# Two output biases of a four-stage transformer kernel: from a VectorE addition to a one-row TensorE product

## What is computed

```python
def _L0_xattn_ref(q, k, v, ...):          # 16 heads, an extra position term in the scores ("cope")
    ...
    return out @ Wo_w.T + Wo_b
def _L1_xattn_ref(q, kv, ...):            # 16 heads, plain
    ...
    return out @ w_out + b_out
...
x = x + tanh(g_xattn[0]) * _L0_xattn_ref(layernorm(x), ctx, ctx, ...)
x = x + tanh(g_ffn[0])   * _L0_ffn_ref(layernorm(x), ...)
x = x + tanh(g_xattn[1]) * _L1_xattn_ref(layernorm(x), ctx, ...)
x = x + tanh(g_ffn[1])   * _L1_ffn_ref(layernorm(x), ...)
```

## Time and profile before

| | us |
|---|---|
| median of 3 runs | 4901.44 |
| lowest and highest | 4898.19, 4908.12 |
| the profiled execution | 4907.68 |
| its span, first to last instruction | 4906.0 |
| VectorE busy in it | 3975.6 (81%) |
| TensorE busy in it | 3332.2 (68%) |
| ScalarE busy in it | 2426.4 (49%) |
| GpSimd busy in it | 1394.9 (28%) |

### The profile page before, as it was taken

One profiled execution on the slowest core, in us unless ns is written; L12 is line 12 of the kernel. 1 busy time (PEld: TensorE's weight loads), 2 busy tenths in 40 slices (PEclk: granted clock), 3 DMA queues, 4 the chain that ended last, 5 costly groups with the idle time before them and its releaser, 6 DMA issues.

```text
span 4906.0 us, 64542 instructions
## 1 busy us (share of the span) xinstructions
PE 3332.2 (68%) x21126; PEld 2210.1 (45%) x21126; DVE 3975.6 (81%) x8619; ACT 2426.4 (49%) x5505; POOL 1394.9 (28%) x1125
## 2 busy tenths in 40 slices
PE   3347677676767767676776767767676766767686
PEld 2125344453544436354453635435354443635363
DVE  3699787887978879787888978888797887978753
ACT  2464555545555454554545455554554545455432
POOL 0242322323232232322323232232323223232300
PEclk7558687686877778687786867778687777868687
DMA  4000000000000000000000000000000000000000
GB/s 130 13 5 1 1 12 1 11 1 1 12 1 12 1 11 1 1 12 1 11 1 3 10 1 12 1 11 1 1 12 1 12 1 11 1 1 7 1 7 3
DMA packets 42692, 40.93 MB, mean 8 GB/s; under 512 B 6469, under 2 KB 42343, under 8 KB 42361
## 3 DMA queue, kind: packets, MB, share of 16 engines
q1 hardware_dynamic: 42360, 36.85, 2.5%
HBM read 32.64 MB, written 4.19 MB: 8 GB/s over the span
## 4 chain that ended last, share of the span: by engine, by line
DVE 42%; PE 26%; ACT 13%; issue 13%; POOL 2%; DVEq 0%; POOLq 0%; ACTq 0%; DMA 0%; SPq 0%
DVE banks L731 7%; DVE u L962 5%; PE banks L288 4%; DVE row_negmax L1273 4%; PE banks L366 3%; PE banks L275 3%; DVE masks L722 3%; PE banks L297 3%; DVE eg_eth L980 3%; DVE c L689 3%; DVE o L989 2%; PE banks L330 2%; DVE steps L749 2%; PE banks L810 2%; ACT core_prob L581 2%
## 5 line engine op out<-in xcount | busy, mean ns | idle before, releaser
L731 DVE COPY_PREDICATED banks<-masks,banks 128x448 f32<-128x448 int16 (+5 forms) x1536 | 1030.6, 671 | 36.6
L632 POOL TENSOR_TENSOR steps<-slope,rises 128x512 f32<-128x512 f32 x256 | 301.3, 1177 | 2373.9 <-DVE masks L722 2162.0
L810 PE MATMUL banks<-xn,w 128*128 128x256 f16 x6912 | 876.7, 290 | 74.6 <-ACT h L882 50.0
L810 PEld LDWEIGHTS banks<-xn,w 128*128 128x128 f16 x6912 | 704.9, 104 | 239.4 <-ACT h L882 58.2
L689 DVE TENSOR_TENSOR_SCAN c<-gate,cap 128x514 f32<-128x514 f32 x256 | 371.0, 1449 | 83.6 <-POOL neg_rest L642 82.4
L1273 DVE TENSOR_REDUCE row_negmax<-banks 128x4 f32<-128x1024 f32 x256 | 297.3, 1216 | 154.5 <-PE banks L351 151.9
L722 DVE TENSOR_SCALAR masks<-shift 128x512 int16<-128x512 int16 x1536 | 334.3, 288 | 89.8 <-ACT shift L558 85.6
L823 PE MATMUL banks<-w,a 128*128 128x256 f32 x1152 | 303.6, 411 | 85.3 <-DVE o L989 79.0
L646 POOL TENSOR_TENSOR partial<-partial,core_scores 128x512 f32<-128x512 f32 x256 | 361.4, 1412 | 0.1
L642 POOL TENSOR_TENSOR neg_rest<-shift,c 128x512 f32<-128x512 bf16 x256 | 293.5, 1146 | 219.6 <-ACT shift L570 144.5
L882 ACT ACTIVATE h<-banks,b 128x256 f32<-128x256 f32 x576 | 239.8, 467 | 198.3 <-PE banks L810 197.3
(11 more groups left out here) (262 smaller groups left out, 7493.4 us busy)
## 6 DMA issues: line engine op xcount, KB each, us to landing
stage<-in_L_ffn_w SPq DMA_DIRECT2D x16, 512.0 KB, 5.5
ahead<-in_ctx SPq DMA_DIRECT2D x32, 128.0 KB, 2.2
ahead<-in_x SPq DMA_DIRECT2D x32, 128.0 KB, 2.3
u<-in_ctx SPq DMA_DIRECT2D x32, 128.0 KB
x<-in_x SPq DMA_DIRECT2D x32, 128.0 KB
out<-x SPq DMA_DIRECT2D x32, 128.0 KB, 1.8
stage<-in_L_ffn_w SPq DMA_DIRECT2D x8, 256.0 KB, 6.1
stage<-in_L_ffn_sw SPq DMA_DIRECT2D x2, 512.0 KB, 4.4
```

Source lines behind the costliest of these rows:

```text
L731: move = nc.vector.copy_predicated(tab[:, :, 0:S - b], k.masks[:, n, :, 0:S - b], tab[:, :, b:S])
L810: last = nc.tensor.matmul(k.bank[bank][:, f * S:(f + 1) * S], w[:, e, a, c, par, f * P:(f + 1) * P], k.x_parts[:, b, c, :], start=(n == 0) ...
```

## The change

`token_projection` can now add a bias in PSUM: after the two products of a token tile it multiplies a stationary operand of one row and 128 columns (`half[0:1, 0:1]`, the constant 0.5, broadcast) with the first row of the bias tile (1 x 256), accumulating into the same bank. That is two further products in float32 for each call, for cope and for cross, 64 in all 32 calls. `add_to_x` loses its second instruction. The bias rows of these two stages are scaled by 2.0 ahead of the batches, in place of the tanh, so that 0.5 times the row is the bias, and the tanh comes in with the first instruction of `add_to_x`, which multiplies the whole bank by it. The gated stage keeps its bias on VectorE.

```diff
-def token_projection(nc, w, src, bank):
+def token_projection(nc, w, src, bank, ones=None, row=None):
     for t in range(NT):
         for c in range(NC):
             last = nc.tensor.matmul(bank[:, t * D:(t + 1) * D], src[:, c, t * P:(t + 1) * P], w[:, c, :],
-                                    start=(c == 0), stop=(c == NC - 1))
+                                    start=(c == 0), stop=(c == NC - 1 and row is None))
+        if row is not None:
+            last = nc.tensor.matmul(bank[:, t * D:(t + 1) * D], ones[0:1, 0:1].broadcast_to([1, P]), row[0:1, :],
+                                    start=False, stop=True)
     return last
...
-    token_projection(nc, k.wo_cope, k.oT, k.bank[7]).then_inc(sem["tail_y_done"], 1)
+    token_projection(nc, k.wo_cope, k.oT, k.bank[7], k.half, k.bo_cope).then_inc(sem["tail_y_done"], 1)
...
-    add_to_x(nc, k, step, k.bank[7], k.tanh_g[:, 0:1], k.bo_cope)
+    add_to_x(nc, k, step, k.bank[7], k.tanh_g[:, 0:1])
...
-def add_to_x(nc, k, step, bank, scale, bias_row):
+def add_to_x(nc, k, step, bank, scale):
     x = k.norm.x
     step(nc.vector.scalar_tensor_tensor(whole(x), bank[:], scale, whole(x), ALU.mult, ALU.add))
-    step(nc.vector.tensor_tensor(x[:], x[:], bias_row[:].unsqueeze(1).broadcast_to([P, NT, D]), ALU.add))
...
-    token_projection(nc, w.wo, k.oT, k.bank[7]).then_inc(sem[p + "y_done"], 1)
+    token_projection(nc, w.wo, k.oT, k.bank[7], k.half if kind == "cross" else None,
+                     w.tbo if kind == "cross" else None).then_inc(sem[p + "y_done"], 1)
...
-        add_to_x(nc, k, step, k.bank[7], k.tanh_g[:, 1:2], w.tbo)
+        add_to_x(nc, k, step, k.bank[7], k.tanh_g[:, 1:2])
...
-                for n, b in ((0, k.bo_cope), (1, k.bo_cross), (3, k.bo_gated)):
-                    nc.vector.tensor_scalar(b[:], b[:], k.tanh_g[:, n:n + 1], None, ALU.mult)
+                for b in (k.bo_cope, k.bo_cross):
+                    nc.vector.tensor_scalar(b[:], b[:], 2.0, None, ALU.mult)
+                nc.vector.tensor_scalar(k.bo_gated[:], k.bo_gated[:], k.tanh_g[:, 3:4], None, ALU.mult)
```

## The result

The changed kernel takes 4929.90 us (median of five runs, 4924.53 to 4937.11), the kernel before 4907.42 on the same chip (five runs, 4898.19 to 4910.11): ratio 1.0053, 95% interval 1.0037 to 1.0068. It is slower, by 22.5 us between the medians; the ratios here are taken over the runs and not from two medians. The forecast was 4906 with a range to 4919, so it was wrong. The profiled execution of after has 4924.53, its span is 4922.6, against 4906.0.

A forecast was written before the change was run, and what follows sets the result against it. VectorE was taken to wait for TensorE at both places; cope +10.8, cross -7.2 and the last cross +1.1 gave +4.7 us, from the median 4901.44 to 4906.1, forecast as 4906, range 4894 to 4919.

The forecast's parts named there:

- What bounds the kernel: At the additions to x in cope and cross VectorE waits for TensorE; the removed additions are on the path, 34.6 us.
- What is added: Four more records per call in cope and cross, 0.252 each: 1.01 us at the high clock, 1.80 at the low.
- first rival: One-row products in cope and cross do not overlap with neighbours: four cost 1.52 or 2.54, +24, 4926 us; chance 0.10.
- The rule that I set beside this step: On the added products: row count does not matter for weight-load time; by it the sum would be some 2 us lower.
- Which clock: Behind cope's addition 0.50 in four batches, 0.61 to 0.68 in five, 0.97 to 1.00 in seven; cross 1.00 in 15.
- all low: Cope falls in the low clock in all batches, or L321's slack is used up in more: +11.2, 4913 us; chance 0.10.
- a longer run of products may bring the clock up earlier: In cope's low-clock batches, set against about 1 us of waiting at L321; both counted as nothing.
- What is late next: Behind cope, VectorE's slack at L321 shrinks by 0.72, about 1 us of waiting over four low-clock batches, counted as nothing.
- Cross: In cross, 15 batches of 1.01 added less 1.49 removed, -7.2 us; the last batch at the low clock, +1.1.
- The sum: Over all batches: cope +10.8, cross -7.2, the last cross +1.1, together +4.7 us.

The follow-up runs named there:

- the version with 128 rows: Changed kernel with its bias products, still behind each token tile, given 128 rows instead of one, bias scaled by 2/128: 4891.53 us, 0.9961 against before.
- the two second profiles: The kernel before and the changed kernel, each run once more unchanged for another profile: 4903.0 us (ratio 0.9984) and 4918.89 us (1.0018).
- cross alone: One-row bias products in cross only, cope keeping VectorE's addition as in the kernel before: 4915.81 us, ratio 1.0011 against before.
- cope alone: One-row bias products in cope only, cross keeping VectorE's addition as in the kernel before: 4927.29 us, ratio 1.0030 against before.

## Why the prediction was wrong

**What bounds the kernel: right.** VectorE waits for TensorE at both places. Leaving the biases out took 11.1 us from cope for a computed 11.5, and 1.48 from cross for 1.49 in each of the 14 batches with a high clock, so the instructions removed were on the path. That the total gave 37 for 34.6 is no finer proof, since its rest moved too.

**What is added: wrong in size, and the step that failed is the choice of the nearest row.** I took 0.252 a record from L840, nine rows, and concluded that one-row products overlap. But L840's four records stand among themselves. Nor is 0.252 against 0.230 a difference of rows: four records of 128 rows take 1.13 us too, in the timeline of cross above, and both figures share out a longer first step over three or seven records. What differs here is the neighbour. Measured, four cost 1.44 at the high clock (1.01 forecast) and 2.60 at the low one (1.80). That is the first rival's size, 1.52 and 2.54, and its mechanism in part: a load does not overlap with the product before it where the number of rows changes; between the two records of one product it does. The evidence was in the trace of before, in the weight loads of cope's third batch:

```profile
961.24 0.13 PEld L453 LDWEIGHTS banks<-table,core_queries 64*128 64x128 f16 x2 [1.57 <-ACT slope L605]
961.78 2.96 PEld L297 LDWEIGHTS banks<-wv_cope,ahead 128*128 128x128 f32 x8 [0.41 <-issue]
964.76 0.58 PEld L275 LDWEIGHTS banks<-ident,xn 128*128 128x128 f32 x4
```

From 64 rows to 128 PEld is idle for 0.41 "until issue"; from 128 to 128, to another tile, there is none. The first of these changes is one of the type too, from f16 to f32. Another place of that trace parts the two, at the high clock:

```profile
1261.87 3.14 PEld L810 LDWEIGHTS banks<-xn,w 128*128 128x128 f16 x15
1265.02 0.47 PEld L275 LDWEIGHTS banks<-ident,core_prob 128*128 128x128 f32 x4
1265.66 0.11 PEld L351 LDWEIGHTS banks<-core_keys,core_queries 64*128 64x128 f16 x2 [0.17 <-issue]
1265.98 2.52 PEld L810 LDWEIGHTS banks<-xn,w 128*128 128x128 f16 x24 [0.21 <-issue]
```

From f16 to f32 with 128 rows in both there is no idle time; from 64 rows to 128 within f16 there is, 0.21. So it is the rows and not the type. The trace of before has 919 changes of the row count at which the products follow each other without idle time, and in 918 of them the load starts less than 0.01 us ahead of its product; the other is from 9 rows to 32. The rule that I set beside this step says, in the Trainium skill, TensorE: Matmul & The Clock Gate, Step-by-step: what each phase is for, that the row count does not matter for a load's time. L300's loads agree: at the low clock the first of a pair took 283 ns and the second 333, and with 128 rows the first took 285 and the second 333. The same section of the Trainium skill lets a load be pulled ahead if the row groups don't conflict or it goes to the background buffer; no load was pulled ahead across a change of rows in the stretches shown here, so the price lay in the neighbourhood and not in the load.

**Which clock: wrong.** The clock mix was taken over from before: four batches low, five in the middle, seven high. It was all low, 16 of 16. With four at 2.60, cope is 16 x 2.60 - 11.5 = +30.1, and +30.7 was measured. I had both halves, as two rivals of 0.10 each: "all low" with my price, +11.2, and the rival's price with my mix, +24. I treated them as independent draws, "a shifted program draws anew", but the change itself moves the clock, and both came together. I had also written that a longer run of products may bring the clock up earlier; with 128 rows that is what happens, with the interleaved row the opposite.

**What is late next: wrong.** The slack at L321, 0.65 in the third batch, was to shrink by 0.72, with about 1 us of waiting in all, counted as nothing. The 0.72 was right, as the version with 128 rows shows (0.65 left of 1.38, and a wait in the last batch alone, where before has one too). What failed is the clock again: in the changed kernel the list behind the product ran on at the low clock, so the slack was gone in all 16 batches and VectorE waited there 11.2 us. The norm behind cope cost 10.2: the term that I had set to nothing is larger than the whole forecast sum.

**Cross: the same term, mis-sized.** Forecast were -7.2 and +1.1, measured +1.9 over the 16 batches (+0.1 between the two second profiles), and with cross alone nothing measurable in the total. Where the clock is high it is 1.44 - 1.49, about even; one batch fell in the low clock, 7.85 for 4.95, and the other 15 are 1.0 below before in sum. VectorE's idle time ahead of the addition is 2.82 where I expected 2.35.

**The sum.** By the sections the change costs 42.8 us against the forecast sum of 4.7. Of the 38.1 between them, 6.5 are the clock in cope at my price, 12.8 the price there, some 8.0 cross, 10.2 the norm, and 0.6 is left over. Of the 42.8, 17.1 are left in the profiled execution, so the total looks closer to the forecast than the mechanism was. The 25.7 between them lie in the rest. Most of what can be placed is between cross's first row maxima and its first `rsum`: 653.4 (650.1 in the second profile of after), 672.3 and 670.6 in the two of before. There VectorE waits for the last weighing products, fifth batch, before and after:

```profile
1731.66 1.52 PE L375 MATMUL banks<-ident,u 128*128 128x128 f32 x8
1732.85 0.26 DVE L1294 RECIPROCAL rsum<-banks 128x16 f32<-128x16 f32 x1 [3.10 <-PE banks L375]
```

```profile
1733.76 1.09 PE L378 MATMUL banks<-ident,u 128*128 128x128 f32 x8
1734.52 0.26 DVE L1297 RECIPROCAL rsum<-banks 128x16 f32<-128x16 f32 x1 [1.58 <-PE banks L378]
```

The eight records take 1.52 us before and 1.09 after, and the wait is 3.10 and 1.58: the clock rises at another point of the batch. Over the batches this wait sums to 59.7 us before and 45.9 after (58.8 and 47.7 in the second profiles). It repeats in the second profile of after, and in part with cope alone (663.9), so it hangs on the changed program and not on one execution. Why the lower clock in cope should give back time more than 100 us later in the batch I could not settle. The rest ranges from 4177 to 4215 over all kernels run, 7 apart between two profiles of the same one, and nothing here predicts it. The same holds for the 18 us by which the rest of the 128-row kernel (4186.9) is below that of before: only 4 of its 22 us are in the sections, so the part of its gain that the mechanism explains for certain is its distance from after, 36 us in cope and cross.

## What to carry to other kernels

Look at the neighbours of a small product, not at its size: in a row of full products, a bias of one row costs a stall at each change (here 0.19 us at the high clock, 0.30 at the low one), and a constant operand with all 128 rows (scaled by 1/128, the bias row being on all partitions anyway) costs no more and none of the stalls. Put it first, in one piece, ahead of the wait for the data, where it fills an idle gap: that took the same idea from 0.5% slower to 1.1% faster. And where the clock changes within a stage, price an added piece of TensorE work with the clock that it will itself bring about, for which both levels are to be carried through to the end with the slack behind them.

## What the runs showed of the hardware

- A change of the number of rows between neighbouring stationary operands leaves PEld idle: between 128 and 1, either way, 0.33 us at granted clock 1.00 and 0.65 at 0.50, which lengthens the product by 0.19 and 0.30; from 64 to 128, in f16, it was 0.21 at 1.00, and 0.41 at 0.50. Neighbours with 128 rows each have none of it, whether of different tiles or of different types. The one change without it in the trace of before is from 9 rows to 32, once ahead of the batches; it is so in every other trace too, and why is open.
- One-row pieces among cope's full products came with a granted clock of 0.50 until 5.4 us behind the addition in 16 of 16 batches, in each of three profiles. The same with 128 rows had reached 1.00 by then in 16 of 16, and one row in one piece at the head too. The Trainium skill, TensorE: Matmul & The Clock Gate, What's actually happening, lets activity release the clock; these runs don't speak against that, since the clock rose behind work in all forms, and add that the bias product with 128 rows and with one row takes the same 1.9 us but the clock had risen before the addition behind the first in 16 batches, behind the second in three.
- The addition of 128x512 took 0.69 alone and 1.45 beside GpSimd. Removed at both places, it was worth 20.8 us in cross and 11.1 in cope: the company in which an instruction runs counted for more than which stage it was in.
